# Attention from the longest tile to the shortest, values halved around the first scores, four hidden pieces moved forward

## The chip, the core and the metric

The kernel runs on one core of a Trainium2 chip. The metric is device microseconds of one launch; each number is a median of several runs. The core has five engines that run their own instruction lists and meet only at semaphores: TensorE (PE; matrix products and transposes into PSUM, a memory of eight banks of 128 x 512 float32), VectorE (DVE), ScalarE (ACT), GpSimd (POOL) and SyncE (SP, which starts most DMAs).

## The reference, cut to what matters

Two layers over 2048 tokens of width 128. Each computes `x + attention(layernorm(x)) + ffn(layernorm(x))`. The first layer (a recurrent memory and one selected expert) takes the first 95 us or so and isn't touched. The second one is

```python
xn = _layernorm(x, axis=-1)
q, k, v = xn @ wq, xn @ wk, xn @ wv            # one head of width 128
q, k = rope(q), rope(k)                        # half of the columns are rotated
s = (q @ k.T) / 128 - 1e30 * mask              # causal, 2048 x 2048
attention = softmax(s) @ v @ wo
h = silu(xn @ w1.T * s1) * (xn @ w2.T * s2)    # 512 wide, ternary weights
h = gelu(h @ h1.T * sh1)                       # 512 x 512
h = gelu(h @ h2.T * sh2)                       # 512 x 512
ffn = h @ w3.T * s3
```

## The kernel before, in words

The 2048 tokens are 16 tiles of 128. Tile t attends to the t + 1 blocks 0 to t, four blocks to a group: 40 groups and 136 blocks in all. Products of the feed-forward part are made in float16, each operand in a high and a low part, so each has a high and a low matmul.

**Rope and values** (to about 113 us). For each of four chunks of 512 tokens PE makes the turned, swapped and skipped parts of queries and keys (L733 to L739), DVE multiplies by the tables (L1774, L1776) and adds for the queries (L1778, counted in `turned_dve`), POOL adds for the keys (L1326, `turned_pool`), and ACT copies the unrotated half (L1166, L1167, `skip_act`). Then `values(c)` for c = 0 to 3 makes the value blocks, already multiplied by wo (L745); DVE copies the first two (L1782), ACT the last two (L1178).

**The attention loop** runs over tiles t = 0 to 15, and one more time for what is left. In step t the engines do the following, each in the order given.

- PE: `scores(t)` (L793, the mask L795), each group in a bank of `SCORE_BANK`, when the exponential that read this bank is done; `turn_round(t-1)` transposes the first two groups of exponentials (L804) into bank 4 or 5; the early `gated(u)` of the step; then for each group of tile t-1 `weighted` (the product with the values, L813, into bank 7) and the next `turn_round`. The late gates of the step stand ahead of the last `weighted`.
- ACT: copies the transposed groups back to SBUF (L1217), tanh of the early gates (L1190), exponentials of tile t with their row sums (L1233; each needs the bias from DVE and is followed by a short accumulator read), the remaining copies, high copies (L1241, float16 high part of a gate's result) of the first 12 gates, tanh of the late gates, and `weights(i)`: a square (L1205) and, from i = 2 on, two float16 copies (L1210, L1211).
- DVE: maxima of the score groups of tile t (L1809), their maximum and the bias (L1814, L1816), the early gates (L1793, L1794, and from gate 12 on the high copy, a cast, L1801), the closing of tile t-1 (L1832, L1833, L1835), the late gates, and a ternary check of weights (L1842).
- POOL: ahead of the loop the low parts of x (`xL`, four of L1311 and L1312 in 512 columns). Then for each gate of step t, in order, the low part of its result (L1311, L1312, 256 columns) after its high copy, and for weights of the step two 512-column operations (L1346, L1347).

A gate is one 128 x 256 piece of the first feed-forward layer. There are 32, two per step: both early up to step 11, one early and one late from step 12. Gate u uses bank 3 or 6 and waits until the gate before it in this bank is done (`GATE_AFTER`, `hA_ready`). Its buffer is one of six, so DVE's gate u waits for POOL's low part of gate u-6.

The 11 blocks of weights are converted and tested for being ternary during the loop, two per step: block i on ACT in step i // 2 + 9, on POOL one step later and on DVE two steps later (`weights_with`).

**The hidden stage** follows: two layers of 16 pieces, each eight matmuls of 512 columns (L855 high, L856 low) into bank u % 8, with two Gelus on ACT (L1259, L1260) and the low part on DVE (L1862, L1864). The last layer and the output follow. ACT's first Gelu waits for all low parts of gates and for all ternary checks.

Of the kernel before, what the change touches and what calls it, by code (L numbers as in the profile page):

```python
# [6 lines left out]
ALU = mybir.AluOpType  # L7
# [48 lines left out]
ACT_HIGH = 12  # L56
WT_TILE = 9
# [26 lines left out]
def program(nc, a, out):  # L84
    with ExitStack() as ctx:
# [163 lines left out]
        def weights_with(t):  # L249

            return [i for i in range(NWT) if i // 2 + WT_TILE == t]

# [68 lines left out]
        def groups_of(t):  # L321
            before = sum((u + 4) // 4 for u in range(t))
            return [(before + k, c, min(4, t + 1 - c)) for k, c in enumerate(range(0, t + 1, 4))]


        FULL = 3 * NT // 4
        SCORE_BANK = [gi % (3 if t < FULL else 4) for t in range(NT) for gi, _, _ in groups_of(t)]
# [4 lines left out]
        PER = NU // NT  # L332
        assert PER == 2
        GATE_EARLY = [range(PER * t, PER * t + (2 if t < FULL else 1)) if t < NT else () for t in range(NT + 1)]
        GATE_LATE = [range(GATE_EARLY[t].stop, PER * t + PER) if t < NT else () for t in range(NT + 1)]
        GATE_BANK = [3 if u % PER and u // PER < FULL else 6 for u in range(NU)]
        GATE_AFTER = [max([w for w in range(u) if GATE_BANK[w] == GATE_BANK[u]], default=None) for u in range(NU)]

# [108 lines left out]
        def _(pe):  # L447
# [293 lines left out]
            def values(c):  # L741
                b = (4, 0, 5, 1)[c]
# [13 lines left out]
            for c in range(4):  # L756
                values(c)

            def gated(u):
# [4 lines left out]
                if u == 0:  # L764
                    pe.wait_ge(w16_ready, 4)
                if u % (2 * HT4) == 0:
                    pe.wait_ge(xl_ready, u // (2 * HT4) + 1)
# [6 lines left out]
            def scores(t):  # L774

                if t % 4 == 0:

                    pe.wait_ge(skip_act, t // 2 + 2)
                    pe.wait_ge(turned_dve, t // 4 + 1)
                    pe.wait_ge(turned_pool, t // 4 + 1)  # L780
                    pe.wait_ge(v1_act, max(t // 4 + 1, 2))
                if t == 0:
                    pe.wait_ge(mask_act, 2)
                if t == FULL:

                    pe.wait_ge(hA_ready, PER * FULL)
                for gi, c, cnt in groups_of(t):
# [5 lines left out]
                    i = mm(PS[:, k, 0:cnt * P], qT1[:, t * P:(t + 1) * P], kT1[:, c * P:(c + cnt) * P], start=True, stop=not last)  # L793
                    if last:
                        i = mm(PS[:, k, (cnt - 1) * P:cnt * P], ident_b, causal_b, start=False, stop=True)  # L795
                    i.then_inc(s_done, 1)

            def turn_round(t, gi, c, cnt):

                pe.wait_ge(p_ready, gi + 1)  # L800
                if gi >= 2:
                    pe.wait_ge(pt_act, gi - 1)
                for b in range(c, c + cnt):
                    i = tr(PS[:, 4 + gi % 2, (b - c) * P:(b - c + 1) * P], Pr[t % 2][:, b * P:(b + 1) * P], ident)  # L804
                i.then_inc(pt_done, 1)

            def weighted(t, gi, c, cnt):

                pe.wait_ge(pt_act, gi + 1)
                if c == 0:  # L810
                    (pe.wait_ge(pv_read, t) if t else pe.wait_ge(reach_ready, 2))
                for b in range(c, c + cnt):
                    i = mm(PS[:, 7, (t % 4) * D:(t % 4 + 1) * D], PT[t % 2][:, b * P:(b + 1) * P], V1[:, b, :], start=(b == 0), stop=(b == t))  # L813
                if c + cnt > t:
                    i.then_inc(pv_done, 1)

            for t in range(NT + 1):
                if t < NT:
                    scores(t)
                groups = groups_of(t - 1) if t else []  # L820
                for g in groups[0:2]:
                    turn_round(t - 1, *g)
                if t < NT:
                    if t == 0:

                        pe.wait_ge(skip_act, 8)
                        pe.wait_ge(rope_dve, 8)
                        pe.wait_ge(v1_act, 4)

                        pe.wait_ge(sums_ready, 2)  # L830
                        mm(PS[:, 7, 0:2], ones, sums, start=True, stop=True).then_inc(sums_done, 1)
                for u in GATE_EARLY[t]:
                    gated(u)
                for k, g in enumerate(groups):
                    if k + 1 == len(groups):
                        for u in GATE_LATE[t]:
                            gated(u)
                    weighted(t - 1, *g)
                    if k + 2 < len(groups):
                        turn_round(t - 1, *groups[k + 2])  # L840

            pe.wait_ge(w16_ready, 2 * NWT)
            pe.wait_ge(pv_read, NT)
            for layer, (wH, wL, sH, sL, done, read) in enumerate(((h1H, h1L, hAH, hAL, g1_done, g1_act), (h2H, h2L, hBH, hBL, g2_done, g2_act))):
                for ch in range(4):
                    cols = slice(ch * BANK, (ch + 1) * BANK)
                    (pe.wait_ge(low_ready, 4 * ch + 4) if layer else pe.wait_ge(gate_low, NU // 4 * (ch + 1)))
                    for m in range(HT4):
                        u = 4 * ch + m
                        if u >= 8:  # L850
                            pe.wait_ge(read, u - 7)
                        elif layer:
                            pe.wait_ge(g1_act, 8 + u + 1)
                        for k in range(HT4):
                            mm(bank(u % 8), wH[:, k, m * P:(m + 1) * P], sH[:, k, cols], start=(k == 0), stop=False)  # L855
                            i = mm(bank(u % 8), wL[:, k, m * P:(m + 1) * P], sL[:, k, cols], start=False, stop=(k == HT4 - 1))  # L856
                        i.then_inc(done, 1)

            for n in range(NT):
# [8 lines left out]
                y = PS[:, n // 4, (n % 4) * P:(n % 4 + 1) * P]  # L868
# [34 lines left out]
        def _(act):  # L903
# [271 lines left out]
            act.wait_ge(v1_act, 2)  # L1175
            for c in range(2, 4):
                act.wait_ge(v1_done, c + 1)
                f(V1[:, 4 * c:4 * c + 4, :].rearrange("p n d -> p (n d)"), bank((4, 0, 5, 1)[c]), ACT.Copy).then_inc(v1_act, 1)  # L1178
            act.wait_ge(xt2_act, 4)
            for c in range(1, 4):  # L1180
                high(c)

# [30 lines left out]
            def turned_back(t):  # L1213

                for gi, c, cnt in groups_of(t):
                    act.wait_ge(pt_done, gi + 1)
                    f(PT[t % 2][:, c * P:(c + cnt) * P], PS[:, 4 + gi % 2, 0:cnt * P], ACT.Copy).then_inc(pt_act, 1)  # L1217
                    yield

            for t in range(NT + 1):  # L1220
                copies = turned_back(t - 1) if t else iter(())
# [712 lines left out]
```

## Time and profile before

| | us |
|---|---|
| median of 3 runs (279.24 to 279.93) | 279.56 |
| the profiled execution | 279.73 |
| its span, first to last instruction | 277.8 |
| PE busy | 261.5 (94%) |
| DVE busy | 216.4 (78%) |
| ACT busy | 193.8 (70%) |
| POOL busy | 100.7 (36%) |
| first scores of the loop on PE | 113.48 |
| first hidden product on PE | 210.27 |

A PE matmul's shown duration includes its way through the array, and matmuls follow each other faster than that; so PE's prices are read from start to start. A float32 product shows as two records. Shown durations of ACT overlap too.

### The profile page before, as it was taken

Reading aid. Unit: us, or ns where it says so; the run is one execution under the profiler, and the core shown is the slowest. Engines: PE = TensorE matmul, PEld = TensorE weight load, DVE = VectorE, ACT = ScalarE, POOL = GpSimd, SP = SyncE. Lnnn points to the kernel's source line nnn. Section 1 sums busy time; section 2 is a strip of 40 time slices with the busy share of each in tenths; the row PEclk is TensorE's granted clock in tenths of the full one; section 3 lists DMA queues with packets and bytes.
Section 4 is the critical chain, followed back from the end, with each engine's and each line's share of the span. In section 5 each row is a group of like instructions: output and inputs, shape, how many; then the busy total and the mean of one; then the engine's idle time right before and its main releaser. Section 6 shows DMA issues by size and latency. Waiting matters only on the chain.

```text
span 277.8 us, 5424 instructions
## 1 busy us (share of the span) xinstructions
PE 261.5 (94%) x1798; PEld 169.0 (61%) x1802; DVE 216.4 (78%) x734; ACT 193.8 (70%) x473; POOL 100.7 (36%) x129
## 2 busy tenths in 40 slices
PE   7899899999979699899999999999999999999993
PEld 2379845466654445657777777778695444444482
DVE  6977489999997689589999878877943766666684
ACT  1487489885555569678856799999674877777730
POOL 9314000000000058988874389989871000000000
PEclk9999999999999999999999999999999999999998
DMA  7700000000000380400000000000000000000005
GB/s 200 207 13 2 2 0 4 1 0 0 2 2 0 113 343 2 151 2 4 0 2 0 2 0 1 4 0 0 2 0 2 0 0 1 2 1 0 0 17 139
DMA packets 8288, 8.51 MB, mean 31 GB/s; under 512 B 1730, under 2 KB 7363, under 8 KB 7747
## 3 DMA queue, kind: packets, MB, share of 16 engines
q1 hardware_dynamic: 7826, 7.84, 8.9%
q8 instruction: 16, 0.26, 0.4%
q10 hardware_dynamic: 432, 0.30, 0.4%
q14 instruction: 14, 0.11, 0.1%
HBM read 7.09 MB, written 1.05 MB: 29 GB/s over the span
## 4 chain that ended last, share of the span: by engine, by line
PE 75%; DVE 16%; ACT 4%; issue 2%; DMA 2%; SPq 0%; DVEq 0%; ACTq 0%
PE PS L855 10%; PE PS L856 10%; PE PS L813 10%; PE PS L793 9%; PE PS L804 4%; PE PS L627 3%; PE PS L489 3%; PE PS L508 3%; PE PS L574 3%; PE PS L454 2%; PE PS L770 2%; PE PS L771 2%; DVE arena L1559 2%; DMA x<-L_attn_x 2%; PE PS L474 1%
## 5 line engine op out<-in xcount | busy, mean ns | idle before, releaser
L855 PE MATMUL PS<-arena 128*128 128x512 f16 x128 | 48.5, 379 | 0.6 <-issue 0.6
L856 PE MATMUL PS<-arena 128*128 128x512 f16 x128 | 48.5, 379 | 0.0
L1862 DVE TENSOR_TENSOR arena<-arena 128x512 f32<-128x512 f32 x32 | 22.2, 693 | 19.5 <-ACT arena L1260 19.5
L793 PE MATMUL PS<-arena 128*128 128x512 f32 (+3 forms) x80 | 32.0, 531 | 0.0
L1259 ACT ACTIVATE arena<-PS,arena 128x512 f32<-128x512 f32 x32 | 22.0, 688 | 13.2 <-PE PS L856 13.2
L1319 POOL CAST arena<-arena 128x512 f16<-128x512 f32 x2 | 1.2, 608 | 73.1 <-ACT x L1121 73.1
L1311 POOL TENSOR_TENSOR arena<-arena 128x256 f32<-128x256 f32 x32 | 21.5, 673 | 15.6 <-DVE arena L1801 13.6
L1233 ACT ACTIVATE arena<-PS,lnt 128x512 f32<-128x512 f32 (+3 forms) x40 | 24.9, 634 | 2.3 <-DVE lnt L1816 2.2
L1312 POOL TENSOR_TENSOR arena<-arena,small 128x256 f16<-128x256 f32 (+1 forms) x36 | 23.8, 660 | 2.8
L1809 DVE TENSOR_REDUCE mxb<-PS 128x1 f32<-128x512 f32 (+3 forms) x40 | 22.1, 601 | 1.6 <-PE PS L795 1.6
L855 PEld LDWEIGHTS PS<-arena 128*128 128x128 f16 x128 | 12.5, 98 | 15.7 <-issue 0.7
L1260 ACT ACTIVATE arena<-PS,arena 128x512 f16<-128x512 f32 x32 | 21.8, 681 | 0.0
L856 PEld LDWEIGHTS PS<-arena 128*128 128x128 f16 x128 | 12.5, 98 | 15.0
L793 PEld LDWEIGHTS PS<-arena 128*128 128x128 f32 x80 | 14.0, 190 | 11.8 <-issue 9.0
L804 PE MATMUL PS<-con,arena 128*128 128x128 f32 x136 | 19.6, 274 | 0.5 <-ACT arena L1233 0.5
L813 PE MATMUL PS<-arena,xn 128*128 128x128 f32 x144 | 19.3, 279 | 0.4 <-ACT xn L1217 0.2
L813 PEld LDWEIGHTS PS<-arena,xn 128*128 128x128 f32 x144 | 17.4, 191 | 1.4 <-ACT xn L1217 1.1
L454 PE MATMUL PS<-warm 128*128 128x512 bf16 x44 | 14.0, 442 | 4.0 <-DVE arena L1578 1.6
L813 PE MATMUL PS<-arena 128*128 128x128 f32 x128 | 17.3, 279 | 0.3 <-ACT arena L1217 0.2
L804 PEld LDWEIGHTS PS<-con,arena 128*128 128x128 f32 x136 | 15.1, 141 | 3.6 <-issue 1.7
L1793 DVE SCALAR_TENSOR_TENSOR arena<-arena,PS 128x256 f32<-128x256 f32 x32 | 13.4, 420 | 4.6 <-ACT arena L1190 3.9
L1794 DVE SCALAR_TENSOR_TENSOR arena<-PS,arena 128x256 f32<-128x256 f32 x32 | 15.5, 484 | 1.1
(287 smaller groups left out, 636.6 us busy)
## 6 DMA issues: line engine op xcount, KB each, us to landing
arena<-h_T SPq DMA_DIRECT2D x2, 1024.0 KB, 5.5
x<-L_attn_x SPq DMA_DIRECT2D x4, 256.0 KB, 4.6
arena<-cos SPq DMA_DIRECT2D x1, 1024.0 KB, 4.8
arena<-sin SPq DMA_DIRECT2D x1, 1024.0 KB, 6.9
out<-arena SPq DMA_DIRECT2D x4, 256.0 KB, 2.3
arena<-w_T SPq DMA_DIRECT2D x3, 256.0 KB, 3.0
con<-shape_constants ACTq DMA_DIRECT2D x1, 192.0 KB, 3.4
w1e<-L_ffn_W SPq DMA_DIRECT2D x1, 128.0 KB
```

Of the source, the lines that this page charges most:

```text
L793: i = mm(PS[:, k, 0:cnt * P], qT1[:, t * P:(t + 1) * P], kT1[:, c * P:(c + cnt) * P], start=True, stop=not last)
L804: i = tr(PS[:, 4 + gi % 2, (b - c) * P:(b - c + 1) * P], Pr[t % 2][:, b * P:(b + 1) * P], ident)
L813: i = mm(PS[:, 7, (t % 4) * D:(t % 4 + 1) * D], PT[t % 2][:, b * P:(b + 1) * P], V1[:, b, :], start=(b == 0), stop=(b == t))
L855: mm(bank(u % 8), wH[:, k, m * P:(m + 1) * P], sH[:, k, cols], start=(k == 0), stop=False)
L856: i = mm(bank(u % 8), wL[:, k, m * P:(m + 1) * P], sL[:, k, cols], start=False, stop=(k == HT4 - 1))
L1233: f(Pr[t % 2][:, c * P:(c + cnt) * P], PS[:, SCORE_BANK[gi], 0:cnt * P], ACT.Exp, scale=1.0 / D, bias=nbs[:, t:t + 1], accum_out=rsums[:, ...
L1259: f(FP[u % 4], bank(u % 8), ACT.Gelu, scale=s_[:, u % HT4:u % HT4 + 1])
L1260: f(high, bank(u % 8), ACT.Gelu, scale=s_[:, u % HT4:u % HT4 + 1]).then_inc(read, 1)
L1311: o.need(o.did(tt(rest, value, high, ALU.subtract)))
L1312: return tt(low, rest, low_scale.broadcast_to([P, cols]), ALU.mult)
L1809: i = did(v.tensor_reduce(mxb[:, gi:gi + 1], PS[:, SCORE_BANK[gi], 0:cnt * P], AX.X, ALU.max))
L1862: v.tensor_tensor(RP[m], FP[m], high, ALU.subtract).then_inc(rest_ready, 1)
```

## The change

1. `TILE` runs from 15 down to 0. A step's index is now called i; it is the place in the order, and t = TILE[i]. Counters of groups follow the place.
2. The values of chunks 2 and 3 come after the first scores on PE (with the sums, which move to bank 4); ACT copies one, after its remaining high parts of x, and DVE the other, ahead of its first gate.
3. The first scores wait for all turned queries and group by group for the turned keys.
4. Gates are no longer two per step: none early and one late in place 0, two in places 1 to 4, four in 5 and 6, three in 7 to 10, two in 11, one in 12. Up to gate 8 all use bank 6. High copies by ACT end with gate 10, and the high copy of a late gate is made one place later (`HIGH_AT`).
5. Weights go one block per place from place 1.
6. Four pieces of the first hidden layer stand in places 13 to 16, between the transposes and the products of the tile before; the banks of the hidden stage are taken in another order (`HIDDEN_BANK`).

```diff
-ACT_HIGH = 12
-WT_TILE = 9
+ACT_HIGH = 11
+WT_TILE = 1
...
-            return [i for i in range(NWT) if i // 2 + WT_TILE == t]
+            return [i for i in range(NWT) if i + WT_TILE == t]
...
+        TILE = [*range(NT - 1, -1, -1)]
+        def groups_of(i):
+            t, ahead = TILE[i], sum((u + 4) // 4 for u in TILE[:i])
+            return [(ahead + k, c, min(4, t + 1 - c)) for k, c in enumerate(range(0, t + 1, 4))]
+        FOUR = NT // 4
+        SCORE_BANK = [(gi + 1) % 4 if i < FOUR else gi % 3 for i in range(NT) for gi, _, _ in groups_of(i)]
...
+        EARLY_GATES, LATE_GATES = (0, 1, 1, 1, 1, 2, 2, 2, 2, 2, 2, 1, 1, 0, 0, 0, 0), (1, 1, 1, 1, 1, 2, 2, 1, 1, 1, 1, 1, 0, 0, 0, 0, 0)
+        GATES_AT = [sum(EARLY_GATES[:i] + LATE_GATES[:i]) for i in range(NT + 1)]
...
+        U3 = GATES_AT[FOUR + 1]
+        GATE_BANK = [(6, 3)[u % 2] if u >= U3 else 6 for u in range(NU)]
...
+        HIGH_AT = [(*(GATE_LATE[i - 1] if i else ()), *GATE_EARLY[i]) for i in range(NT + 1)]
+        HIDDEN_BANK = (3, 6, 2, 0, 1, 4, 5, 7)
+        AMONG = {NT - 3: 0, NT - 2: 1, NT - 1: 2, NT: 3}
...
 # PE
-            for c in range(4):
+            for c in range(2):
                 values(c)
...
+            def scores(i):
+                t = TILE[i]
+                for gi, c, cnt in groups_of(i):
+                    k = SCORE_BANK[gi]
+                    if i == 0:
+                        if c == 0:
+                            pe.wait_ge(mask_act, 2)
+                            pe.wait_ge(skip_act, 8)
+                            pe.wait_ge(turned_dve, 4)
+                        pe.wait_ge(turned_pool, c // 4 + 1)
+                        if k == 0:
+                            pe.wait_ge(v1_act, 2)
...
+            def hidden_piece(layer, u):
...
+                elif u == 0:
+                    pe.wait_ge(w16_ready, 2 * NWT)
+                    pe.wait_ge(hA_ready, NU)
+                elif b < 3:
+                    pe.wait_ge(p_ready, max(gi for gi, k in enumerate(SCORE_BANK) if k == b) + 1)
+                elif b == 4:
+                    pe.wait_ge(pt_act, len(SCORE_BANK))
+                elif b == 7:
+                    pe.wait_ge(pv_read, NT)
+                for k in range(HT4):
+                    mm(bank(b), wH[:, k, m * P:(m + 1) * P], sH[:, k, cols], start=(k == 0), stop=False)
+                    i = mm(bank(b), wL[:, k, m * P:(m + 1) * P], sL[:, k, cols], start=False, stop=(k == HT4 - 1))
+                i.then_inc(done, 1)
+
+            for i in range(NT + 1):
+                if i < NT:
+                    scores(i)
+                groups = groups_of(i - 1) if i else []
                 for g in groups[0:2]:
+                    turn_round(i - 1, *g)
+                if i == 0:
+                    pe.wait_ge(sums_ready, 2)
+                    mm(PS[:, 4, 0:2], ones, sums, start=True, stop=True).then_inc(sums_done, 1)
+                    for c in range(2, 4):
+                        values(c)
+                for u in GATE_EARLY[i]:
                     gated(u)
+                if i in AMONG:
+                    hidden_piece(0, AMONG[i])
                 for k, g in enumerate(groups):
                     if k + 1 == len(groups):
+                        for u in GATE_LATE[i]:
                             gated(u)
+                    weighted(i - 1, *g)
                     if k + 2 < len(groups):
+                        turn_round(i - 1, *groups[k + 2])
+                if i == 0:
+                    for u in GATE_LATE[0]:
+                        gated(u)
...
 # ACT, at the end of a place's exponentials and copies
-                for u in GATE_EARLY[t]:
+                for u in HIGH_AT[i]:
                     if u < ACT_HIGH:
                         act.wait_ge(hA_ready, u + 1)
                         f(hAH[:, u % HT4, u // HT4 * ZC:(u // HT4 + 1) * ZC], ZA[u % NZ], ACT.Copy).then_inc(gate_high, 1)
-                for u in GATE_LATE[t]:
+                for u in GATE_LATE[i]:
                     tanh(u)
-                for i in weights_with(t):
-                    weights(i)
+                for w in weights_with(i):
+                    weights(w)
...
 # DVE, at the end of a place
+                for w in weights_with(i - 2):
+                    dve.wait_ge(wc_ready, w + 1)
+                    v.tensor_reduce(tern[:, w:w + 1], WC[w % NWC], AX.X, ALU.max, apply_absolute_value=True).then_inc(tern_ready, 1)
```

POOL's list isn't edited. It reads the same tables: for each place the parts of its gates, then the weights of the place before.

## Rows read from the trace of the kernel before

**Rows 1.** The page, chain that ended last: shares of the span by engine.
```profile
PE 75%; DVE 16%; ACT 4%; issue 2%; DMA 2%; SPq 0%; DVEq 0%; ACTq 0%
```

**Rows 2.** Windows: stretch, length, busy us of each engine, clock, DMA.
```profile
125.20:163.50 38.30, 38.29 (x256) 29.73 (x257) 35.28 (x99) 28.75 (x79) 25.49 (x41) 1.00 0.01 1
163.50:210.27 46.77, 45.89 (x322) 37.04 (x321) 34.49 (x87) 39.11 (x94) 40.26 (x43) 1.00 0.00 1
```

**Rows 3.** Waits, 113 to 210.3 us: who waited, for whom, us, times, longest.
```profile
POOL arena L1311 <- DVE arena L1801: 13.6, 12, 3.3
```

**Rows 4.** Timeline of PE, steps 12 and 13: start us, us, line, operation.
```profile
168.62 3.04 PE L793 MATMUL PS<-arena 128*128 128x512 f32 x8
...
171.55 1.04 PE L804 MATMUL PS<-con,arena 128*128 128x128 f32 x8
172.43 0.27 PE L770 MATMUL PS<-arena 128*128 128x256 f16 x1
...
172.87 1.14 PE L813 MATMUL PS<-arena,xn 128*128 128x128 f32 x8
173.84 0.60 PE L804 MATMUL PS<-con,arena 128*128 128x128 f32 x4
```

**Rows 5.** Timeline of PE, first matmuls of hidden pieces 0 and 1.
```profile
210.27 0.38 PE L855 MATMUL PS<-arena 128*128 128x512 f16 x1 [0.56 <-issue]
...
212.00 0.38 PE L855 MATMUL PS<-arena 128*128 128x512 f16 x1
```

**Rows 6.** Timeline of PE, the four values blocks.
```profile
109.91 3.73 PE L745 MATMUL PS<-arena,xT 128*128 128x128 f32 x32
```

**Rows 7.** Timeline of POOL: gate parts, weights, and a part before weights.
```profile
122.03 0.67 POOL L1311 TENSOR_TENSOR arena<-arena 128x256 f32<-128x256 f32 x1
122.78 0.61 POOL L1312 TENSOR_TENSOR arena<-arena,small 128x256 f16<-128x256 f32 x1
123.53 0.67 POOL L1311 TENSOR_TENSOR arena<-arena 128x256 f32<-128x256 f32 x1
...
171.52 1.28 POOL L1346 TENSOR_TENSOR arena<-arena 128x512 f32<-128x512 f32 x1
...
174.11 1.27 POOL L1346 TENSOR_TENSOR arena<-arena 128x512 f32<-128x512 f32 x1
...
205.58 0.67 POOL L1311 TENSOR_TENSOR arena<-arena 128x256 f32<-128x256 f32 x1 [1.53 <-DVE arena L1801]
...
206.90 1.26 POOL L1346 TENSOR_TENSOR arena<-arena 128x512 f32<-128x512 f32 x1
```

**Rows 8.** Timeline of DVE, step 8 and two checks; all casts: min/median/max ns.
```profile
136.88 0.42 DVE L1793 SCALAR_TENSOR_TENSOR arena<-arena,PS 128x256 f32<-128x256 f32 x1
...
140.02 0.14 DVE L1832 TENSOR_REDUCE lnt<-rsums 128x1 f32<-128x2 f32 x1
...
140.66 1.28 DVE L1809 TENSOR_REDUCE mxb<-PS 128x1 f32<-128x512 f32 x2
...
142.28 0.42 DVE L1793 SCALAR_TENSOR_TENSOR arena<-arena,PS 128x256 f32<-128x256 f32 x1
...
178.34 1.27 DVE L1842 TENSOR_REDUCE small<-arena 128x1 f32<-128x512 f32 x2
...
L1801 DVE CAST arena<-arena x20: 294/470/891, 137.9 to 205.2; 128x256 f16<-128x256 f32 x20
```

**Rows 9.** Timeline of ACT: copies, exponentials and a tanh, back to back.
```profile
172.19 1.09 ACT L1217 ACTIVATE xn<-PS 128x512 f32<-128x512 f32 x2
...
175.63 0.69 ACT L1233 ACTIVATE arena<-PS,lnt 128x512 f32<-128x512 f32 x1
...
176.29 0.38 ACT L1233 ACTIVATE arena<-PS,lnt 128x128 f32<-128x128 f32 x1
...
176.63 0.49 ACT L1190 ACTIVATE arena<-PS,arena 128x256 f32<-128x256 f32 x1
```

**Rows 10.** The page, groups: the first Gelu of each hidden piece.
```profile
L1259 ACT ACTIVATE arena<-PS,arena 128x512 f32<-128x512 f32 x32 | 22.0, 688 | 13.2 <-PE PS L856 13.2
```

More of the change, by code:

```diff
@@ L765, in gated @@
                     pe.wait_ge(w16_ready, 4)
+                if u == U3:
+                    pe.wait_ge(p_ready, max(gi for gi, b in enumerate(SCORE_BANK) if b == 3) + 1)
                 if u % (2 * HT4) == 0:
@@ L792, in scores, with turn_round @@
                     last = c + 4 > t
-                    i = mm(PS[:, k, 0:cnt * P], qT1[:, t * P:(t + 1) * P], kT1[:, c * P:(c + cnt) * P], start=True, stop=not last)
+                    n = mm(PS[:, k, 0:cnt * P], qT1[:, t * P:(t + 1) * P], kT1[:, c * P:(c + cnt) * P], start=True, stop=not last)
                     if last:
-                        i = mm(PS[:, k, (cnt - 1) * P:cnt * P], ident_b, causal_b, start=False, stop=True)
-                    i.then_inc(s_done, 1)
-            def turn_round(t, gi, c, cnt):
+                        n = mm(PS[:, k, (cnt - 1) * P:cnt * P], ident_b, causal_b, start=False, stop=True)
+                    n.then_inc(s_done, 1)
+            def turn_round(i, gi, c, cnt):
                 pe.wait_ge(p_ready, gi + 1)
+                if gi == 0:
+                    pe.wait_ge(reach_ready, 2)
                 if gi >= 2:
@@ L814, in weighted @@
                 if c + cnt > t:
[L815 to L820, printed above, removed]
-                for g in groups[0:2]:
[L822 to L831, printed above, removed]
-                for u in GATE_EARLY[t]:
+                    n.then_inc(pv_done, 1)
@@ new lines, in hidden_piece @@
+            def hidden_piece(layer, u):
+                wH, wL, sH, sL, done, read = ((h1H, h1L, hAH, hAL, g1_done, g1_act), (h2H, h2L, hBH, hBL, g2_done, g2_act))[layer]
+                ch, m, b = u // HT4, u % HT4, HIDDEN_BANK[u % 8]
+                cols = slice(ch * BANK, (ch + 1) * BANK)
+                if m == 0:
+                    (pe.wait_ge(low_ready, 4 * ch + 4) if layer else pe.wait_ge(gate_low, NU // 4 * (ch + 1)))
+                if u >= 8:
+                    pe.wait_ge(read, u - 7)
+                elif layer:
+                    pe.wait_ge(g1_act, 8 + u + 1)
+                elif u == 0:
[11 more added lines that the diff above has]
+                i.then_inc(done, 1)
@@ L842, in _ @@
[L842 to L857, printed above, removed]
+                        turn_round(i - 1, *groups[k + 2])
@@ L859, in _ @@
+                if i == 0:
+                    for u in GATE_LATE[0]:
+                        gated(u)
+            for layer in range(2):
+                for u in range(4 * HT4):
+                    if layer or u >= len(AMONG):
+                        hidden_piece(layer, u)
             for n in range(NT):
@@ L1174, in _ @@
                     f(causal_b, con[:, C_CAUSAL:C_CAUSAL + P], ACT.Copy).then_inc(mask_act, 1)
[L1175 to L1178, printed above, removed]
             act.wait_ge(xt2_act, 4)
@@ L1181, in _ @@
                 high(c)
+            act.wait_ge(v1_done, 3)
+            f(V1[:, 8:12, :].rearrange("p n d -> p (n d)"), bank(5), ACT.Copy).then_inc(v1_act, 1)
             def tanh(u):
@@ L1258, in _ @@
                         act.wait_ge(rest_ready, piece - 3)
-                    f(FP[u % 4], bank(u % 8), ACT.Gelu, scale=s_[:, u % HT4:u % HT4 + 1])
-                    f(high, bank(u % 8), ACT.Gelu, scale=s_[:, u % HT4:u % HT4 + 1]).then_inc(read, 1)
+                    f(FP[u % 4], bank(HIDDEN_BANK[u % 8]), ACT.Gelu, scale=s_[:, u % HT4:u % HT4 + 1])
+                    f(high, bank(HIDDEN_BANK[u % 8]), ACT.Gelu, scale=s_[:, u % HT4:u % HT4 + 1]).then_inc(read, 1)
             def network():
@@ L1801, in gate @@
                     v.tensor_copy(hAH[:, m, c * ZC:(c + 1) * ZC], ZA[u % NZ]).then_inc(gate_high, 1)
-            for t in range(NT + 1):
-                if t < NT:
-                    groups = groups_of(t)
+            for i in range(NT + 1):
+                if i < NT:
+                    groups = groups_of(i)
                     for gi, c, cnt in groups:
                         dve.wait_ge(s_done, gi + 1)
-                        i = did(v.tensor_reduce(mxb[:, gi:gi + 1], PS[:, SCORE_BANK[gi], 0:cnt * P], AX.X, ALU.max))
-                    need(i)
+                        n = did(v.tensor_reduce(mxb[:, gi:gi + 1], PS[:, SCORE_BANK[gi], 0:cnt * P], AX.X, ALU.max))
+                    need(n)
                     g0, g1 = groups[0][0], groups[-1][0]
@@ L1870, in _ @@
                 w = ysc[:, b * BANK:(b + 1) * BANK]
-                need(did(v.tensor_tensor(w.rearrange("p (n e) -> p n e", n=4), bank(b).rearrange("p (n e) -> p n e", n=4),
+                need(did(v.tensor_tensor(w.rearrange("p (n e) -> p n e", n=4), bank(HIDDEN_BANK[b]).rearrange("p (n e) -> p n e", n=4),
                                          s3.unsqueeze(1).broadcast_to([P, 4, D]), ALU.mult)))
```

105 lines of the change are left out of this document (42 added, 63 removed).

## The prediction, made before the changed kernel ran

> **What bounds the kernel now.** I read the chain of waits first: TensorE (PE) holds 75% of it [rows 1]. Then the busy time by stretch: from 125.2 to 163.5 us PE is busy 38.29 of 38.30 us and from 163.5 to 210.27 us 45.89 of 46.77, while VectorE (DVE), ScalarE (ACT) and GpSimd (POOL) each have slack in at least one of the two [rows 2]. POOL's slack is what matters here. In the waits, its gate parts wait 13.6 us for DVE's casts [rows 3], so before, POOL had its work early enough and was waiting for more.
>
> Start-to-start prices of PE [rows 4]: scores of 13 blocks with the mask 171.55-168.62 = 2.93 us, so 0.22 per block and 0.06 for the mask; eight transposes 0.88, 0.11 each; one gate 0.44; four value products (eight records) 0.97, a semaphore included, so about 0.22 each. Over the 136 blocks and 32 gates of the stage that is 136 x (0.215+0.11+0.222) + 16 x 0.06 + 32 x 0.44 = 89.4 us in the 96.9 us from the first scores (113.4) to the first hidden product at 210.27 [rows 5]. So 7.5 us is the most that a better order can win on PE.
>
> I call a step of the loop a place (0 to 16); place i holds the scores of tile 15-i and the rest of tile 16-i. Before, place and tile are the same.
>
> **PE's side of the change.** The work is the same; the last two values blocks (1.8 us) move behind the first scores, and four hidden pieces move in. A piece is eight matmuls, 212.00-210.27 = 1.73 us [rows 5]. The first two values blocks take half of the 3.73 us at 109.91 [rows 6], so scores of tile 15 start at 111.8 instead of 113.4. They take 3.5 us, and the last reduce and the bias 0.9: first exponential at about 117 (bias 116.4, but ACT also copies a values bank). Place 1 starts on PE at 117.4. Pure PE sums for places 1 to 4 are 9.5, 9.0, 8.4 and 7.9 us (15 to 12 blocks of scores, 16 to 13 of the rest, two gates). If PE alone decided, the stage with its four pieces would be 111.8 + 89.4 + 1.8 + 6.9 = 209.9, and with 3 us of stalls (my choice: under half of the 7.5 now, since the tiny tiles that wait for gates at the start get pieces between them) 212.9; four pieces being done, that equals a hidden start at 206.0: 4.3 us earlier than 210.27.
>
> **Prices of the others.** POOL, start to start [rows 7]: gate part after gate part 123.53-122.03 = 1.50 us; gate part to weights 206.90-205.58 = 1.32; one set of weights 174.11-171.52 = 2.59. DVE [rows 8]: two gates with casts 140.02-136.88 = 3.14, so 1.57 each (1.0 without cast); a tile's closing 0.64; reduces and bias of nine blocks 1.62, 0.135 per block more or less; two ternary checks 1.27, 0.6 each. ACT [rows 9]: exponential of four blocks 0.66, of one 0.34; copy of four blocks about 0.5; tanh 0.36, and I take the same for a high copy of the same size.
>
> **A new circle through four engines.** A late gate's high copy is now made on ACT one place later, behind that place's exponentials (HIGH_AT). Weights go one per place from place 1: ACT's square at w+1, POOL at w+2 behind that place's gate parts, DVE's ternary check at w+3, ahead of the next place's reduces. So in place 3 DVE ends with check 0, which needs POOL's weights 0, which stand behind the part of gate 4 (late gate of place 2), which needs the high copy behind the exponentials of place 3. Before, no check stood within this circle (weights began at place 9, high copies by ACT ended with gate 11 in place 5). Length in place 3: exponentials and two copies 3.1, high copy 0.4, part 1.3, weights 2.6, check 0.6, reduces and bias of 12 blocks 2.3, handing over 0.2 = 10.5 us, against 8.4 of PE. In place 4 it is about 9.9 against 7.9. Step by step I get place starts on PE at 117.4, 127.4, 136.3, 144.7, 154.3 (places 1 to 5), the exponentials of places 3, 4 and 5 at 141.0, 151.5 and 161.4, and the high copy of gate 8 at 164.1 (161.4 + three exponentials and a copy 2.3 + 0.4).
>
> **The backlog on POOL.** Until then POOL can have done only gates 0 to 7 and weights 0 and 1: of the 42 us from the end of its last xL part (122.0) to 164.1 it works 8 x 1.5 + 2 x 2.6 = 17 and idles 25. From 164.1 it has gates 8 to 31 and weights 2 to 10 left: 24 x 1.50 - 9 x 0.18 + 9 x 2.59 = 57.7 us, ending at 221.8. This is the term that decides. Is it ever starved again? DVE for places 6 to 12: 19 gates with casts 29.8, reduces and biases of 49 blocks 9.4, seven closings 4.5, seven checks 4.2 = 47.9, from 168.9 (check 2 waits for weights 2 at 168.1) to 216.8, with about 1.5 of waits for checks 218.3. So DVE and POOL run side by side, each just ahead of the other's need, and POOL stays full. PE has only 38 us of work for these seven places and waits. In place 13 DVE's check 10 stands ahead of the reduces of tile 1, so tile 1 waits for the end of POOL's work.
>
> The Trainium skill (Perfetto Trace Analysis, GPSIMD Engine Instruction) says to time GpSimd by the spacing of starts rather than by reported spans. By the reported spans (0.67 + 0.61 per part, 2 x 1.27 per weights) the backlog would be 53.8 us and the result 286.8; the trace agrees with the page where POOL is never idle (1.50 against 1.28), so I use the spacing.
>
> **The tail.** From 221.8: check 0.6, reduce and bias 0.6, exponential with its accumulator read 0.65, two transposes 0.25, hidden piece 2 1.73, value products 0.45, transpose 0.15, hidden piece 3 1.73, last product 0.2: hidden piece 4 starts at 228.2. Less the four pieces done (6.9) that is 221.3, against 210.27: **+11.0 us**. Pieces 0 and 1 lie in waits of PE; 2 and 3 don't, and they would have to run anyway. Behind it the stage is as before: ACT now waits 13.2 us for PE there [rows 10], so its late first Gelu (about 228 with the table load) is caught up; piece 8 needs it only at 235. The new bank order is free: each piece's bank is released by work already waited for.
>
> Edits that I cost at nothing: the longer wait before the first scores for all turned queries and keys (they are done by about 111.3, under the values; if not, 1 us); the sums in bank 4; the values copy moved to DVE (0.7, under the first exponentials; at worst 0.7); one high copy moved from ACT to DVE (0.5 on DVE, within the sum above). Each lies between 0 and its own duration, none below. SP's load of the second hidden weights waits for the turned keys as before, at about 112.5, and is first read in place 8, some 60 us later.
>
> Profiled execution: 279.73 (span 277.8) + 11.0 = 290.7. It stands 0.17 above the median of 279.56, so about **290.5**.
>
> **The rivals.**
> 1. PE decides after all, faster: 279.6 - 4.3 = 275.3. For it: PE's 75% and the tiny tiles' idle time. Against it: it needs POOL to have 57.7 us of work done between place 5 and the end, some 50 us on PE's clock.
> 2. DVE alone decides, with no backlog on POOL (high copies come early enough): DVE's first reduce of place 5 at 154.4, then places 5 to 12 with 8.2 + 47.9 us: reduces of tile 2 begin at 210.5. The last three tiles take 9.5 from there (three pieces 5.2, the rest 4.3): hidden piece 4 at 220.0, +2.8: 282.5. Against it: the order on ACT puts the high copies behind the exponentials.
> 3. The circle doesn't delay, the backlog is there. The earliest for gate 8's high copy: place 5 at 152.2, bias 3.2 later, 2.8 more: 158.2, 5.9 earlier than above: 284.6. This is also the lower end of the main mechanism; POOL at its reported spans (4 us less, 286.8) lies between the two.
> 4. Casts get slower since POOL is never idle. The casts of before take 0.29 to 0.89 us, median 0.47 [rows 8]; at 0.24 more each, some 0.7, DVE is 4.6 us later over 19 gates, passes POOL, and the end is 3 to 4 us later: 294. It decides when a cast costs more than 0.15 above that median. The Trainium skill (SBUF — State Buffer, Who interferes with whom) says that a DVE operation in a two-port mode and a GpSimd operation exclude each other for their whole length; by that rule this case would be the likelier the fuller POOL is.
> 5. No change: the gain of 4.3 and a smaller loss cancel, 279.6.
> The granted clock is 1.00 in both stretches of [rows 2]; with PE idle a third of places 8 to 13 it could fall for a while, which would double the two last pieces: +3, inside case 4.
>
> **How the numbers follow.** Main case 0.58 (290.5, own range 287.5 to 293); case 1 0.07; case 2 0.09; case 3 0.11; case 4 0.12; case 5 0.03. The range 282 to 295 takes in cases 2, 3 and 4 and leaves out about 0.15. Within 0.3% (0.8 us) is about what a measurement of this kernel tells from no change: 0.03; faster 0.07; slower 0.90.
>
> **What would show it.** Right: POOL near full from about 164 to 222 and mostly idle from 122 to 164; its last weights at about 220; DVE waiting for POOL at the ternary checks in places 3 to 5 and 13; PE's waits in places 6 to 14 summing to some 15 us; the first scores about 1.6 us earlier; the hidden stage unchanged in pace. Wrong: POOL done well before the tail, high copies of ACT right behind their gates, or PE without gaps from 160 to 215. If DVE's casts average over 0.6 us and POOL waits for DVE late, case 4 holds.

## The result: 4.3% slower, and the profile after

| | before | changed |
|---|---|---|
| median, us | 279.75 | 291.87 |
| range, us | 279.24 to 282.67 | 291.65 to 292.47 |
| ratio, 95% interval | | 1.0426 [1.0382, 1.0470] |
| profiled execution, us | 279.73 | 292.47 |
| its span, us | 277.8 | 290.5 |
| hidden piece 4 starts, less four pieces (6.9) | 210.27 (piece 0) | 229.90 - 6.9 = 223.0 |

The last row carries the whole loss: 223.0 - 210.27 = 12.7 us, as much as the spans differ. So the time was lost ahead of hidden piece 4, and the hidden stage behind it kept its pace. The profiled execution is the slowest of the four; by the medians the loss is 12.1 us. The page of the changed kernel shows where, in 40 slices of 7.26 us. Below are POOL's busy tenths and PE's granted clock.

```profile
POOL 9312000000000559721265389998997000000000
PEclk9999999999999799999997999999999999999998
```

Inside the stage POOL is nearly empty from 123 to 145 us (2, 1, 2), about half busy until 160 (6, 5), and full from about 165. Its timeline from the changed kernel gives the edges. The columns are start, length, line, operation, and in brackets how long POOL was idle before and who ended it.

```profile
121.05 1.04 POOL L1338 TENSOR_TENSOR arena<-arena,small 128x512 f16<-128x512 f32 x1
128.29 0.67 POOL L1337 TENSOR_TENSOR arena<-arena 128x256 f32<-128x256 f32 x1 [6.21 <-ACT arena L1267]
...
137.17 0.67 POOL L1337 TENSOR_TENSOR arena<-arena 128x256 f32<-128x256 f32 x1 [6.01 <-ACT arena L1267]
...
155.76 0.67 POOL L1337 TENSOR_TENSOR arena<-arena 128x256 f32<-128x256 f32 x1 [4.81 <-ACT arena L1267]
...
165.42 0.67 POOL L1337 TENSOR_TENSOR arena<-arena 128x256 f32<-128x256 f32 x1 [4.41 <-ACT arena L1267]
...
222.19 1.26 POOL L1373 TENSOR_TENSOR arena<-arena 128x512 f32<-128x512 f32 x1
```

The row at 165.42 is gate 8's part; from there to 222.19 + 1.26 = 223.45 no row has a bracket: 58.0 us without a gap. The waits of the changed kernel between 110 and 225 us (who waited, for whom, us, times, longest) show who held whom.

```profile
POOL arena L1337 <- ACT arena L1267: 27.1, 5, 6.2
ACT arena L1259 <- DVE lnt L1842: 17.4, 11, 3.2
...
DVE small L1871 <- POOL arena L1373: 9.7, 5, 2.4
```

Where POOL waited 13.6 us for DVE's casts before [rows 3], it now waits 27.1 for ACT's high copies (L1267), and DVE's ternary check (L1871) waits 9.7 for POOL's weights, which it never did before. ACT in turn waits 17.4 for the bias, 11 times; the check explains it only where it waits itself (5 times), elsewhere the bias stands behind the rest of DVE's list. The circle of place 3, one row from each engine in turn (timelines of ACT, POOL and DVE):

```profile
145.17 0.74 ACT L1267 ACTIVATE arena<-arena 128x256 f16<-128x256 f32 x2
...
145.69 0.67 POOL L1337 TENSOR_TENSOR arena<-arena 128x256 f32<-128x256 f32 x1 [5.66 <-ACT arena L1267]
...
147.01 1.27 POOL L1372 TENSOR_TENSOR arena<-arena 128x512 f32<-128x512 f32 x1
148.35 1.27 POOL L1373 TENSOR_TENSOR arena<-arena 128x512 f32<-128x512 f32 x1
...
149.66 0.69 DVE L1871 TENSOR_REDUCE small<-arena 128x1 f32<-128x512 f32 x1 [2.40 <-POOL arena L1373]
150.26 1.88 DVE L1835 TENSOR_REDUCE mxb<-PS 128x1 f32<-128x512 f32 x3
```

The reduces of place 4 start at 150.26, though its scores began on PE at 145.44. PE then had little to do, and its clock fell. Windows of the changed kernel, columns as in [rows 2]; the clock is the column behind POOL:

```profile
150.00:154.00 4.00, 2.04 (x19) 1.80 (x17) 3.54 (x10) 1.55 (x5) 0.87 (x2) 1.00 0.00 0
154.00:158.00 4.00, 4.00 (x17) 2.79 (x18) 1.16 (x3) 3.98 (x11) 2.16 (x3) 0.62 0.00 0
165.42:223.45 58.03, 46.56 (x322) 35.32 (x322) 49.19 (x125) 38.56 (x95) 53.28 (x66) 1.00 0.00 1
```

PE was busy for only half of 150 to 154; in the next 4 us the granted clock was 0.62 of full speed, a stretch at 1.2 instead of 2.4 GHz. The third row is the backlog: POOL 53.28 us busy by its reported spans and in fact gapless, DVE 49.19 of 58.03, PE 46.56 of 58.03, where PE had been busy 98% to 100% [rows 2].

DVE too has hardly a gap in the backlog up to 213 us, and it isn't free of POOL there. Two casts of DVE, each with the POOL operation in which it began (timelines of POOL and DVE of the changed kernel):

```profile
197.01 0.61 POOL L1338 TENSOR_TENSOR arena<-arena,small 128x256 f16<-128x256 f32 x1
197.04 0.73 DVE L1827 CAST arena<-arena 128x256 f16<-128x256 f32 x1
...
204.60 1.27 POOL L1372 TENSOR_TENSOR arena<-arena 128x512 f32<-128x512 f32 x1
205.06 0.97 DVE L1827 CAST arena<-arena 128x256 f16<-128x256 f32 x1
```

Both end 0.15 us behind the end of POOL's operation (197.77 and 197.62, 206.03 and 205.87), and 19 of the 21 casts end 0.14 to 0.16 us behind one. DVE's places of three gates all take 6.97 us (first reduces at 187.62, 194.59, 201.56, 208.53), though their reduces shrink from 1.27 to 1.14 and 1.01 us: the three casts grow from 1.44 to 1.59 and 1.72. So DVE ran at POOL's period without a wait for it that the profile shows. Here that cost little: POOL was the later of the two, and its own places of three gates take 6.90 to 6.92 us in a kernel without casts (all high copies on ACT, below).

In the tail the chain passes from POOL through check 10 to tile 1 (timelines of DVE and PE of the changed kernel):

```profile
223.49 0.69 DVE L1871 TENSOR_REDUCE small<-arena 128x1 f32<-128x512 f32 x1 [2.08 <-POOL arena L1373]
224.09 0.41 DVE L1835 TENSOR_REDUCE mxb<-PS 128x1 f32<-128x256 f32 x1
...
225.40 0.44 PE L816 MATMUL PS<-con,arena 128*128 128x128 f32 x2 [0.42 <-ACT arena L1259]
...
225.68 0.38 PE L851 MATMUL PS<-arena 128*128 128x512 f16 x1
...
229.90 0.38 PE L851 MATMUL PS<-arena 128*128 128x512 f16 x1
```

Hidden piece 2 starts at 225.68, piece 4 at 229.90.

### The profile page after: what moved, and what is told of

Read it like the earlier page. It is cut to its first block, busy times and chain, and to the rows that moved or that the text cites. A ratio compares the mean times of both kernels' runs of the same rounds, so it can differ in the third digit from the quotient of the medians.

```text
span 290.5 us, 5417 instructions
## 1 busy us (share of the span) xinstructions
PE 263.3 (91%) x1798; PEld 170.5 (59%) x1802; DVE 218.2 (75%) x736; ACT 192.8 (66%) x471; POOL 100.7 (35%) x129
## 4 chain that ended last, share of the span: by engine, by line
PE 59%; POOL 17%; DVE 14%; ACT 4%; issue 3%; DMA 1%; SPq 0%; POOLq 0%; ACTq 0%; DVEq 0%
PE PS L852 9%; PE PS L851 9%; POOL arena L1337 5%; PE PS L803 4%; POOL arena L1338 4%; POOL arena L1373 4%; POOL arena L1372 4%; PE PS L826 3%; PE PS L637 3%; PE PS L499 3%; PE PS L518 2%; PE PS L584 2%; ACT arena L1259 2%; PE PS L464 2%; DVE mxb L1835 2%
## 5 line engine op out<-in xcount | busy, mean ns | idle before, releaser
L1259 ACT ACTIVATE arena<-PS,lnt 128x512 f32<-128x512 f32 (+3 forms) x40 | 24.8, 626 | 19.3 <-DVE lnt L1842 17.4
L803 PE MATMUL PS<-arena 128*128 128x512 f32 (+3 forms) x80 | 33.1, 546 | 0.0
L1337 POOL TENSOR_TENSOR arena<-arena 128x256 f32<-128x256 f32 x32 | 21.5, 673 | 29.5 <-ACT arena L1267 27.1
L782 PE MATMUL PS<-arena 128*128 128x256 f16 x64 | 15.8, 278 | 7.3 <-DVE arena L1820 7.3
L1286 ACT ACTIVATE arena<-PS,arena 128x512 f16<-128x512 f32 x32 | 22.4, 699 | 0.0
L803 PEld LDWEIGHTS PS<-arena 128*128 128x128 f32 x80 | 14.5, 198 | 12.5 <-issue 10.7
L826 PE MATMUL PS<-arena,xn 128*128 128x128 f32 x128 | 18.0, 281 | 3.5 <-ACT xn L1243 3.5
L826 PE MATMUL PS<-arena 128*128 128x128 f32 x144 | 19.6, 277 | 0.0
L826 PEld LDWEIGHTS PS<-arena,xn 128*128 128x128 f32 x128 | 16.2, 194 | 4.7 <-ACT xn L1243 4.0
L1864 DVE SCALAR_TENSOR_TENSOR x<-PS,lnt,x 128x128 f32<-128x128 f32 x16 | 5.6, 351 | 17.5 <-PE PS L826 17.2
L826 PEld LDWEIGHTS PS<-arena 128*128 128x128 f32 x144 | 17.8, 192 | 0.9 <-ACT arena L1243 0.3
```

Of the source, the lines that this page charges most:

```text
L803: n = mm(PS[:, k, 0:cnt * P], qT1[:, t * P:(t + 1) * P], kT1[:, c * P:(c + cnt) * P], start=True, stop=not last)
L826: n = mm(PS[:, 7, (t % 4) * D:(t % 4 + 1) * D], PT[i % 2][:, b * P:(b + 1) * P], V1[:, b, :], start=(b == 0), stop=(b == t))
L1259: f(Pr[i % 2][:, c * P:(c + cnt) * P], PS[:, SCORE_BANK[gi], 0:cnt * P], ACT.Exp, scale=1.0 / D, bias=nbs[:, i:i + 1], accum_out=rsums[:, ...
L1286: f(high, bank(HIDDEN_BANK[u % 8]), ACT.Gelu, scale=s_[:, u % HT4:u % HT4 + 1]).then_inc(read, 1)
L1337: o.need(o.did(tt(rest, value, high, ALU.subtract)))
```

## Experiments

The kernel before took 279.7 to 279.8 us beside the experiments, the changed kernel 291.87. Diffs are against it unless said otherwise.

**More POOL work in the idle and in the full stretch.** One operation of a gate part is made twice, 6 us in all, once for gates 0 to 7 and once for gates 16 to 23.

```diff
+                if 0 <= u < 8:        # the other run: 16 <= u < 24
+                    o.need(o.did(tt(zd, ZA[u % NZ], hAH[:, m, cols], ALU.subtract)))
```

> The changed kernel with the first of the two operations of a gate part made twice on POOL for gates 0 to 7: 8 x 0.75 = 6.0 us more work for POOL in the stretch where it idles 27 us. Theory: only parts 4 and 6 lie in the circle, so 0.5 to 2 us slower than the changed kernel. Rival (POOL's total work sets the time): 6 us slower. The result itself is unchanged.

> The same doubling for gates 16 to 23: the same 6.0 us of POOL work, now in the stretch where POOL is never idle. Theory: it all arrives at the end, 5.5 to 6.5 us slower than the changed kernel, about 298. Rivals (DVE or PE decides there and POOL only keeps up): 0 to 2 us slower.

Measured: 293.76 (+1.9) early and 298.16 (+6.3) late. The same work costs three times as much behind 165 us. POOL is the limit there, and not in general.

**All high copies as casts on DVE.**

```diff
-ACT_HIGH = 11
+ACT_HIGH = 0
...
-                    if u == ACT_HIGH:
+                    if u == ACT_HIGH and u:
```

> The changed kernel with all 32 high copies as casts on DVE, right behind each gate, and none on ACT. Theory (backlog on POOL, started by high copies that stand behind the exponentials): gate 8's part can start near 155 us instead of 165.4, and the check no longer waits for a copy behind the exponentials. POOL ends its last weights near 212 instead of 223.5, DVE and POOL then end together, and the time falls by 9 to 11 us, to 281 to 283. Rival A (the order of tiles or its tail costs the time, POOL only follows): within 2 us of 291.9. Rival B (DVE is the limit): ten more casts of about 0.5 us make it slower, 293 to 297.

Measured: 287.89, only 4.0 less than the changed kernel. My number missed by 5 us. The circle was gone: place 5 began on PE at 153.63 instead of 156.13. But then DVE and POOL held each other. Timelines of DVE and POOL in this kernel, start and length:

```profile
177.57 1.27 POOL L1373 TENSOR_TENSOR arena<-arena 128x512 f32<-128x512 f32 x1
178.13 0.86 DVE L1827 CAST arena<-arena 128x256 f16<-128x256 f32 x1
...
179.06 0.67 POOL L1337 TENSOR_TENSOR arena<-arena 128x256 f32<-128x256 f32 x1 [0.23 <-DVE arena L1827]
...
182.10 0.29 DVE L1827 CAST arena<-arena 128x256 f16<-128x256 f32 x1
```

A cast takes 0.29 us when POOL is between operations (182.10). The one at 178.13 begins inside a POOL operation that ends at 178.84 and itself ends at 178.99; then POOL, which had waited for just this cast, starts. The Trainium skill (SBUF — State Buffer, SBUF: two separate sides) describes an exclusive lock on a port pair that GpSimd shares with a DVE operation in a two-port mode, and that whichever starts second waits out. These rows agree; in which mode the cast ran no row shows. A place of three gates took 7.57 us (DVE's first reduces at 182.91, 190.49, 198.06), against 6.97 in the changed kernel, where POOL is behind and never waits for a cast. From the first reduces of place 5 to those of place 13 DVE took 155.94 to 215.29 = 59.4 us, where I had counted 56.1, and check 10 still waited for POOL in the tail. That is 3.3 of the 5 us; PE's granted clock of 0.81 and 0.77 in 208 to 212 and 212 to 216 us may have a part in the rest, which was not tested.

**Ternary checks two places later.**

```diff
-                for w in weights_with(i - 2):
+                for w in weights_with(i - 4):
```

> The changed kernel with DVE's ternary checks two places later, so that no check stands within the circle of exponentials, high copy, gate part, weights and the next reduces. Theory: places 3 to 5 keep PE's pace, gate 8's part starts at about 159.5 instead of 165.4, POOL ends near 217.5; and in the tail tile 1's reduces no longer wait for the last weights, so hidden piece 4 starts near 220 instead of 229.9: 282 to 285. If only the backlog counts and not the circle: 289 to 291 (the tail alone). Rival A (order): within 2 us of 291.9.

Measured: 285.09, 6.8 less, at the edge of what was expected. Now no check waits for POOL. The first scores of places 5 and 6 start at 152.86 and 161.02, and hidden piece 4 at 221.7 instead of 229.9. DVE takes 154.47 to 212.11 = 57.6 us for places 5 to 12, and the last tiles 9.6. These are nearly the times of the prediction's case 2, DVE alone, but not its mechanism. POOL's backlog is still there (timeline of POOL in this kernel, gate 8's part and the last weights):

```profile
160.77 0.67 POOL L1337 TENSOR_TENSOR arena<-arena 128x256 f32<-128x256 f32 x1 [2.52 <-ACT arena L1267]
...
217.50 1.27 POOL L1373 TENSOR_TENSOR arena<-arena 128x512 f32<-128x512 f32 x1
```

It takes 58.0 us again, gapless, and DVE's places of three gates take 6.96 to 6.98 us again, each cast but two ending 0.14 to 0.16 us behind a POOL operation. So POOL still set DVE's pace there through the casts.

**Late high copies ahead of the exponentials.** On ACT:

```diff
+                highs(GATE_LATE[i - 1] if i else ())
                 if i < NT:
...
-                for u in HIGH_AT[i]:
+                highs(GATE_EARLY[i])
```

> The changed kernel with one thing moved: ACT makes the high copies of the late gates of the place before ahead of the exponentials, not behind them. Theory: parts 4, 6 and 8 start some 4 us earlier, check 0 and 1 find their weights done, places 3 to 5 keep PE's pace, gate 8's part starts near 157 and POOL ends near 215. Then DVE and POOL are equal limits and check 10 still holds tile 1: 283 to 286. Rival (the order of tiles or the tail): within 2 us of 291.9.

`highs` is the loop of copies, made a function; the late gates are those of the place before.

Measured: 285.29, 6.6 less. One moved block of copies recovers half of the loss, so their place behind the exponentials was a cause and not a symptom. Gate 8's part starts at 157.94, where the prediction's case 3 had its high copy at 158.2, and the time is near that case's 284.6. The timeline of POOL in this kernel, gate 8's part and the last weights:

```profile
157.94 0.67 POOL L1340 TENSOR_TENSOR arena<-arena 128x256 f32<-128x256 f32 x1 [2.80 <-ACT arena L1250]
...
214.65 1.27 POOL L1376 TENSOR_TENSOR arena<-arena 128x512 f32<-128x512 f32 x1
```

Again 58.0 us from the part (157.94) to the end (215.92): the same backlog, 7.5 us earlier.

**All high copies on ACT, late ones ahead, checks two places later.** The last two edits and

```diff
-ACT_HIGH = 11
+ACT_HIGH = 32
```

> As the run before, and ACT makes all 32 high copies, so that DVE makes no cast, and checks come two places later. Two runs before showed DVE taking 57 us for places 5 to 12 once the backlog is smaller; 21 casts of 0.5 us and their waits for POOL's operations are some 11 to 14 us of it. Theory: DVE falls out, POOL ends near 215 but holds nothing in the tail except its own parts, hidden piece 4 starts near 216 to 219: 278 to 281. If POOL's 58 us of backlog decide alone: 283 to 285. If ACT becomes the limit (ten to twenty more copies of 0.36 us): above 285.

Measured: 281.00, ratio 1.0038 [1.0008, 1.0067] to the kernel before. Without casts DVE is out; POOL still ends at 217.0 and ACT's first Gelu waits 2.3 us for the last check. PE was busy for only 0.80 of the 3 us from 212, and its granted clock was 0.71 and 0.72 in the 6 us behind them. How the distance to the fast version below divides between these wasn't tested.

**Work for the idle POOL.** Late copies ahead and all on ACT as above, checks as in the changed kernel, and

```diff
-            return [i for i in range(NWT) if i + WT_TILE == t]
+            return [i for i in range(NWT) if i // 2 + WT_TILE == t]
...
 # POOL
+                for i in weights_with(t - 1):
+                    weights(i)
                 for u in (*GATE_EARLY[t], *GATE_LATE[t]):
                     gate_parts(u)
-                for i in weights_with(t - 1):
-                    weights(i)
```

> All high copies on ACT, the late ones ahead of the exponentials; weights two blocks per place from place 1; POOL makes the weights of a place ahead of its gate parts; checks as in the changed kernel. So POOL's idle time in places 1 to 5 takes nearly all weights. Theory: POOL's backlog at place 5 shrinks from 58 to about 45 us, it ends before 207, DVE has no casts, PE decides: 275.5 to 279, below the 279.7 of the kernel before. If the order of tiles itself costs time: 283 or more even with POOL and DVE out of the way.

Measured: 278.33, ratio 0.9955 [0.9927, 0.9982]: faster than the kernel before by 0.5%, with an interval clear of 1. It is called the fast version from here on. Windows of this kernel:

```profile
111.50:156.00 44.50, 44.37 (x286) 33.52 (x285) 27.34 (x69) 36.98 (x95) 32.67 (x35) 1.00 0.07 25
156.00:212.00 56.00, 52.89 (x380) 41.64 (x379) 42.95 (x121) 43.81 (x121) 45.06 (x61) 1.00 0.00 1
```

PE is busy 44.37 of 44.50 us and then 52.89 of 56.00. The order of tiles was not at fault: with POOL fed and DVE free of casts, it gains 1.3 us on the kernel before, where the prediction's case 1 had 4.3.

**The other parts of the change.** Pieces taken out of the changed kernel, and out of the fast one (`AMONG = {}`):

> The changed kernel without hidden pieces among the last tiles; all 16 follow the loop, in the same banks. Theory: the pieces stand in PE's waits and save time; without them the last product ends near 227.3 and the hidden stage starts there, where now it stands as if it had started at 223.0: 295 to 297. Rival (the pieces stand ahead of the products and delay the tail): 288 to 291.

> The fast version (work for the idle POOL, 278.3) without hidden pieces among the last four tiles. Theory: with POOL and DVE out of the way the last tiles are a chain of short steps (reduce, exponential, transposes, copy, products), and the four pieces (6.9 us) fill PE's waits in it; without them 3 to 6 us slower, 281 to 284. If PE's clock falls in the gaps, as it did when they were taken from the changed kernel: 285 or more. Rival (the pieces only change places with work behind them): within 1 us.

Measured: 299.49 (+7.6) and 281.93 (+3.6). The second is as expected. The first is 2.5 us beyond, and the windows of the changed kernel without pieces say why:

```profile
212.00:218.00 6.00, 3.27 (x21) 2.47 (x22) 3.87 (x11) 2.86 (x7) 5.54 (x8) 1.00 0.00 0
218.00:224.00 6.00, 3.91 (x17) 2.83 (x16) 2.68 (x7) 1.16 (x3) 4.86 (x5) 0.52 0.00 0
224.00:230.00 6.00, 5.14 (x19) 3.06 (x18) 2.65 (x16) 1.58 (x6) 0.00 (x0) 0.50 0.00 0
```

From 218 to 230 us the clock was at its lower level, 1.2 GHz. In the changed kernel with its pieces it stayed at 1.00 in those 12 us. So the pieces do two things: they use the waits, and they keep PE from being slowed for what follows. How the 7.6 us divide isn't shown. In the fast version the clock stayed at 1.00 from 200 to 224 us without the pieces too, so the clock has no part in its 3.6 us.

Gates flatter in the fast version (three in each of places 5 to 11, two in 12), and all four values ahead of the first scores in the fast version:

```diff
-        EARLY_GATES, LATE_GATES = (0, 1, 1, 1, 1, 2, 2, 2, 2, 2, 2, 1, 1, 0, ...), (1, 1, 1, 1, 1, 2, 2, 1, 1, 1, 1, 1, 0, ...)
+        EARLY_GATES, LATE_GATES = (0, 1, 1, 1, 1, 2, 2, 2, 2, 2, 2, 2, 2, 0, ...), (1, 1, 1, 1, 1, 1, 1, 1, 1, 1, 1, 1, 0, ...)
```

> The fast version with flatter gates: three in each of places 5 to 12, none of them with four or two (EARLY_GATES 2 and LATE_GATES 1 in 5 to 11, 2 and 0 in 12 with two in 12 instead of one). Theory: PE's waits for the bank of a gate (6.1 us, nearly all in places 6 to 10) shrink by a third: 276.5 to 278. If the gates in place 12 push the last low parts: up to 279.

```diff
             for c in range(2):
                 values(c)
+            pe.wait_ge(rope_dve, 6)
+            for c in range(2, 4):
+                values(c)
...
-                    for c in range(2, 4):
-                        values(c)
```

> The fast version with all four value blocks ahead of the first scores, as in the kernel before. Theory: PE starts the first scores 1.8 us later and then has nothing to do while the first exponentials wait for their bias, so 1 to 2 us slower, 279.3 to 280.3. Rival (place 1 waits for the exponentials anyway, which start 1.8 us later, or the start is hidden): 0 to 0.5 us.

The second edit also makes ACT wait for the first two value copies.

Measured: 277.98, ratio 0.9933 [0.9913, 0.9952] for the flatter gates, the fastest of all; its lead of 0.35 us over the run before is within their scatter. Values whole: 280.27 (278.97 to 282.79), 1.9 slower than the fast version as expected, with a scatter that leaves the size open.

**High copies on ACT in the old order** (against the kernel before):

```diff
-ACT_HIGH = 12
+ACT_HIGH = 24
```

> The kernel before, in its old order, with ACT making the high copies of gates 0 to 23 instead of 0 to 11. It tells whether the fast version owes its time to fewer casts rather than to the order of tiles. PE sets the pace there from step 4 on, so within 0.7 us of 279.7. If DVE's casts cost time in the old order too: 278 to 279, and then the order of tiles is worth less.

Measured: 281.13, ratio 1.0053 [1.0032, 1.0074]. Neither number held: it is 1.3 us slower. The waits of this kernel show a new one ahead of POOL's:

```profile
POOL arena L1311 <- ACT arena L1241: 10.5, 4, 3.7
```

POOL's parts wait for ACT's copies, which stand behind the exponentials again. So moving casts to ACT is not a gain by itself: in the old order, with the copies behind the exponentials, it lost 1.3 us. That those waits cost the 1.3 isn't shown. In this profiled execution the first scores started at 114.07, not 113.48, behind a clock of 0.79 in 94 to 102 us. The old order with the copies ahead of the exponentials was not tried, so how much of the fast version's gain belongs to the order of tiles stays open.

## Why the prediction was right, point by point

Forecast 290.5 (282 to 295), measured 291.87. The mechanism was the one forecast: the late high copies, the circle of four engines, POOL's gapless backlog and the tail behind it. More POOL work cost 1.9 us early and 6.3 us late, and moving the copies or the checks out of the circle gave back 6.6 and 6.8 us.

| step | forecast | in the profile |
|---|---|---|
| scores of places 2, 3, 4, 5 start | 127.4, 136.3, 144.7, 154.3 | 127.96, 136.97, 145.44, 156.13 |
| gate 8's part starts on POOL | 164.1 | 165.42 |
| POOL's backlog, gapless | 57.7 | 58.0 |
| from its end to hidden piece 4 | 6.4 | 6.45 |
| loss against the kernel before | 11.0 | 12.7 |

- The circle held, and with its length: first exponentials of places 3, 4 and 5 at 141.79, 152.60 and 162.55, so 10.8 and 9.95 us where I had 10.5 and 9.9.
- The mis-sized term is the start of the backlog, 1.3 us: 0.8 was there by place 3 (the first scores began at 112.1, not 111.8, the first exponential at 117.47, the rest in small stalls), 0.35 came with the circle, 0.15 with the high copy. Much of the 0.8 belongs to the profiled execution and not to the change. Its clock fell ahead of the changed stage (window of the changed kernel, columns as above), and its first scores began at 112.12. In the profiled executions of the experiments, with the same work up to there, they began at 111.33 to 111.65 where that clock was 1.00 (six) and at 111.80 to 112.06 where it was 0.79 to 0.99 (four):

```profile
94.00:102.00 8.00, 5.96 (x17) 2.88 (x18) 6.91 (x38) 5.08 (x13) 4.08 (x4) 0.79 0.88 350
```

- The clock was wrong in place and harmless. I had it falling in places 8 to 13, where it stayed at 1.00; it fell at 154 to 158 us, where the circle had stopped PE. That cost nothing on the path: the reduces of place 5 start at 160.33 right behind check 1 (159.72), not behind their slow scores.
- Spacing of starts on POOL (1.50 and 2.59) was the right price: the reported spans sum to 53.28 in the 58.03 us of the backlog. The prediction's 53.8 and 286.8 for this are a slip; its own terms give 53.6 and 286.6. For the circle the prediction took 2.3 us for the reduces and the bias of 12 blocks, where its price per block gives 2.0; measured were 2.25 (150.26 to 152.51).
- Case 4 had its mechanism right and its outcome wrong. The casts did wait for a full POOL's operations, as the rows of the changed kernel show, but it hardly lengthened them on the whole: the median stayed 0.47 us, the mean rose from 0.50 to 0.56, the longest from 0.89 to 1.22. POOL never waited for DVE behind 165 us. It cost time where it had not been looked for, once POOL had to wait for the casts (casts on DVE).
- Case 3 (backlog without the circle) is what the copies ahead of the exponentials gave: 284.6 forecast, 285.3 measured.
- Case 2's time (282.5) was near what later checks gave (285.1), partly by luck. DVE took 10.9 us for place 5, not 8.2, and 46.7 for places 6 to 12, not 47.9, and POOL's backlog, which the case had away, was there. The rest is scatter: the four runs go from 283.9 to 286.8, the profiled one is 284.1.
- One sign held only in part: checks waited for POOL in places 3, 4, 11, 12 and 13, not in place 5.
- Case 1 (PE decides) needed the repairs on ACT, DVE and POOL. Its price of 4.3 us was too high: the fast versions reach 1.3 to 1.8.
- That PE's waits in places 6 to 14 would sum to some 15 us: in the 58.03 us of the backlog PE was busy 46.56, pieces 0 and 1 among them, so 11.5 idle and 3.5 filled by the pieces.

## What to carry to other kernels

Reordering the longest engine's work moves everyone else's work in time: before doing it, list for each of the other engines what it could have done by a given moment in the new order, and how much is then left. An engine that is 35% busy over the span can be the limit if it idles early and its remainder is longer than what the others have left. When work is queued in an engine's fixed order, look at what stands ahead of a copy or a check that another engine waits for; here one block of copies behind the exponentials cost 6.6 us. And an engine without gaps need not be a limit of its own: look whether the length of its operations follows another engine's.

## What the runs showed of the hardware that I had not expected

- A DVE cast from float32 to float16 in SBUF takes 0.29 us between POOL's operations and up to 1.32 us beside them; it ends 0.15 us behind the POOL operation in which it began. Through this DVE took over POOL's period, 6.97 us per place, while the profile shows DVE busy and no wait.
- PE's granted clock fell to 0.62 in the 4 us behind a stretch with PE busy 2.04 of 4.00 us, and to 0.52 and 0.50 in the 12 us behind one with 3.27 of 6.00; three score records then took 2.58 us from 156.13 on, where the same six together took 2.53 in the kernel with later checks, at full clock. With 6.9 us of matmuls among the last tiles it stayed at 1.00 in those 12 us, and the kernel was 7.6 us faster; the fast version, whose clock fell neither with nor without them, won 3.6.
